# The last adds and their output transfers moved into the LSTM's pass loop

## The reference

```python
lstm_out = _lstm(layernorm(x))                 # 8192 steps, hidden 128
g = argmax(lstm_out @ W_lin.T + b_lin)         # 0 or 1 per step
w = g * lstm_out
inc = cumsum(w)
prefix, suffix = inc - w, inc[-1] - inc
x + 2.0 * lstm_out + prefix * fw_att + suffix * bw_att
```

## Time and profile before

| | us |
|---|---|
| median of 3 runs (lowest, highest) | 1605.08 (1603.58, 1605.31) |
| profiled execution | 1600.95 |
| its span | 1598.9 |
| PE busy | 1511.9 |
| DVE busy | 1369.9 |
| POOL busy | 1123.2 |
| ACT busy | 1040.0 |
| repeated steps of the pass loop | about 1462 to 1574 |
| behind them, to the span's end | 1574 to 1598.9 |

### The profile page before, as it was taken

One profiled execution on the slowest core, in us unless ns is written; L12 is line 12 of the kernel. 1 busy time (PEld: TensorE's weight loads), 2 busy tenths in 40 slices (PEclk: granted clock), 3 DMA queues, 4 the chain that ended last, 5 costly groups with the idle time before them and its releaser, 6 DMA issues. The chain is left out here.

```text
span 1598.9 us, 17964 instructions
## 1 busy us (share of the span) xinstructions
PE 1511.9 (95%) x5006; PEld 772.3 (48%) x5006; DVE 1369.9 (86%) x1623; ACT 1040.0 (65%) x2210; POOL 1123.2 (70%) x536
## 2 busy tenths in 40 slices
PE   8999999999999999999999999999987688999994
PEld 3444444444444444444444444444432235998993
DVE  7406999999999999999999999999988695667998
ACT  3254766667676767675767666676768666777772
POOL 0325989898989898898989898989898761001221
PEclk9999999999999999999999999999989899999997
DMA  9877767677776776777777777776720203000002
GB/s 368 332 251 260 263 225 250 241 254 248 248 262 232 254 246 239 236 253 262 244 254 246 252 249 248 258 243 239 254 97 9 99 1 119 0 0 1 0 0 105
DMA packets 60491, 313.51 MB, mean 196 GB/s; under 512 B 6492, under 2 KB 6544, under 8 KB 27525
## 3 DMA queue, kind: packets, MB, share of 16 engines
q1 hardware_dynamic: 49537, 293.30, 52.8%
q10 hardware_dynamic: 10884, 19.41, 3.8%
HBM read 300.36 MB, written 12.32 MB: 196 GB/s over the span
## 5 line engine op out<-in xcount | busy, mean ns | idle before, releaser
L586 PE MATMUL bank<-ring,xh 128*128 128x512 f32 x2048 | 956.3, 594 | 13.2 <-DVE xh L1179 7.9
L1295 DVE TENSOR_TENSOR_SCAN work<-bank,hstate,work 128x512 f32<-128x512 f32 x512 | 628.1, 1268 | 29.9 <-ACT bank L881 24.4
L586 PEld LDWEIGHTS bank<-ring,xh 128*128 128x128 f32 x2048 | 387.9, 190 | 464.6 <-issue 422.6
L1065 POOL TENSOR_TENSOR work<-work 128x1024 f32<-128x1024 f32 x210 | 495.5, 2359 | 85.6 <-DVE work L1244 77.2
L881 ACT ACTIVATE bank<-work,a_neg 128x512 f32<-128x512 f32 x512 | 344.3, 686 | 226.1 <-DVE work L1295 225.4
L1236 DVE TENSOR_TENSOR work<-work,bank 128x1024 f32<-128x1024 f32 x256 | 310.1, 1217 | 62.0 <-POOL work L1041 50.8
L1244 DVE TENSOR_TENSOR work<-work,bank 128x1024 f32<-128x1024 f32 x168 | 201.2, 1198 | 20.8 <-POOL work L1065 20.8
L480 PE MATMUL bank<-bc_parts,sel 96*128 96x512 bf16 x456 | 172.0, 386 | 28.1 <-DVE work L1236 12.8
L475 PE MATMUL bank<-work,w_sb 128*128 128x512 f32 (+2 forms) x352 | 178.1, 602 | 5.9 <-ACT work L795 2.7
L1140 POOL TENSOR_TENSOR work<-work 128x256 f32 x32 | 28.6, 894 | 215.5 <-ACT work L944 215.5
L1010 POOL TENSOR_TENSOR work<-work 128x1024 f32<-128x1024 f32 x48 | 113.5, 2365 | 18.9 <-ACT work L755 18.7
(11 more groups left out here) (153 smaller groups left out, 1595.4 us busy)
## 6 DMA issues: line engine op xcount, KB each, us to landing
ring<-adj_t SPq DMA_DIRECT2D x256, 1024.0 KB, 5.6
work<-c_scratch ACTq DMA_DIRECT2D x28, 256.0 KB, 5.5
c_two<-c_scratch ACTq DMA_DIRECT2D x28, 256.0 KB, 5.1
xh<-x_rows SPq DMA_DIRECT2D x16, 256.0 KB, 7.0
work<-x_t SPq DMA_DIRECT2D x16, 256.0 KB, 5.4
x_scratch<-work ACTq DMA_DIRECT2D x16, 256.0 KB, 3.8
work<-x_scratch SPq DMA_DIRECT2D x1, 4096.0 KB, 14.1
out_t<-work SPq DMA_DIRECT2D x16, 256.0 KB, 2.4
```

The costliest lines, as they stand in the source:

```text
L586: last = nc.tensor.matmul(mixed[:, :], xn[:, j, :], a, start=(j == 0), stop=(j == BLK - 1))
L1065: nc.gpsimd.tensor_tensor(out=acc, in0=hc[0] if n == 1 else acc, in1=hc[n % 2], op=ALU.add).then_inc(y_added, 1)
L1295: nc.vector.tensor_tensor_scan(hb[s % 2][:, h, :], da[h], dbu[s % 2][:, h, :], hstate[:, HV * s + h:HV * s + h + 1], ALU.mult, ALU.add).th ...
```

## The change

The sixteen last adds move into the While loop: DVE makes eleven of them (chunks 0 to 10), GpSimd five (chunks 11 to 15). For DVE the values are also written to PSUM (`k_bank`), and its adds read them there; GpSimd reads `k_seg` in SBUF. SP gets a While loop of its own, in which it sends the 16 chunks in the order `OUT_ORDER` as they are ready, loads the flag ahead of the last one, and waits for all transfers at the loop's end. In every step GpSimd now also waits that the chunks of the pass before are out (`out_done`, met at once in the first pass). The copies of the states and the count of passes move from the end of the pass to its head, which takes the place of L1337 to L1339; PE's wait for `guess_ready` moves into its loop. The tail's side operations are ordered anew: both selects stand among the comparisons, the rest behind them, `flag` comes later and `k_seg` right behind it.

```diff
@@ -72,6 +72,9 @@
           ("out", 11.5, "post"), ("pcen", 12.5, "post"), ("pvar", 13.5, "post")]
 O_SHARED = 9
 POOL_HC = (1, 3, 8, 10)
+POOL_OUT = (11, 12, 13, 14, 15)
+DVE_OUT = tuple(i for i in range(NC) if i not in POOL_OUT)
+OUT_ORDER = (0, 1, 11, 2, 3, 12, 4, 5, 13, 6, 7, 14, 8, 9, 15, 10)
 C_LOAD = {0: 1, 2: 3, 6: 8, 8: 10}
 PRE_STEPS = sum(s[2] == "pre" for s in SHARED)
 POST_STEPS = sum(s[2] == "post" for s in SHARED)
@@ -252,6 +255,11 @@
         at[0] = pre_only
         o_in = [carve(N // BG).rearrange("p (c t) -> p c t", c=NC // BG) for _ in range(BG)]
+        def last_sum(i, k):
+
+            return (final[:, i, :].rearrange("p (t s) -> p t s", s=SPC),
+                    k[:, i * SPC:(i + 1) * SPC].unsqueeze(1).broadcast_to([P, SEG, SPC]))
+
         def by_chunk_seg(ap):
             return ap.rearrange("p (c s) -> p c s", s=SPC)
@@ -277,6 +285,7 @@
         out_gate = [bank[4], bank[5]]
         l_bank = [bank[6], bank[7]]
         count_ps = bank[6][:, NSEG:NSEG + 1]
+        k_bank = bank[7][:, NSEG:2 * NSEG]
         o_bank = [bank[2]] * O_SHARED + [bank[i] for i in (7, 1, 3, 7, 6, 7, 6)]
...
@@ -410,10 +419,26 @@
             sp.wait_ge(x1_stored, 16 * NC)
             sp.wait_ge(xl_ready, NC)
             sp.dma_start(x1_all, x1_dram.rearrange("c p t -> p c t")).then_inc(x1_in, 16)
-            for i in range(NC):
-                sp.wait_ge(out_ready, i + 1)
-                sp.dma_start(out_t[i], final[:, i, :]).then_inc(out_done, 16)
-            sp.wait_ge(out_done, 16 * NC)
+            sp.sem_inc(out_done, 16)
+            pass_no = sp.alloc_register("sp_pass")
+            go_on = sp.alloc_register("sp_go")
+            sp.reg_mov(pass_no, 0)
+            sp.reg_mov(go_on, 1)
+            with sp.While(lambda: sp.snap(go_on)):
+                pn = sp.snap(pass_no)
+                for i in OUT_ORDER:
+                    if i == OUT_ORDER[-1]:
+                        sp.wait_ge(flag_ready, pn + 1)
+                        sp.sem_inc(flag_seen, 1)
+                        sp.reg_load(go_on, flag[0:1, 0:1])
+                    if i in POOL_OUT:
+                        sp.wait_ge(out_pool, len(POOL_OUT) * pn + (POOL_OUT.index(i) + 1))
+                    else:
+                        sp.wait_ge(out_ready, len(DVE_OUT) * pn + (DVE_OUT.index(i) + 1))
+                    sp.dma_start(out_t[i], final[:, i, :]).then_inc(out_done, 16)
+                sp.wait_ge(out_done, 16 * NC * pn + (16 * NC + 16))
+                sp.sem_inc(flag_seen, 1)
+                sp.reg_add(pass_no, pass_no, 1)
         @block.tensor
@@ -683,9 +708,9 @@
             run_steps(SEG - WARM, -2 * (SEG - WARM), from_zero=True)
             for b in range(2):
                 input_part(0, 0, b)
-            pe.wait_ge(guess_ready, 1)
             with pe.While(lambda: pe.snap(go_on)):
                 pn = pe.snap(pass_no)
+                pe.wait_ge(guess_ready, pn + 1)
                 run_steps(0, 2 * SEG * pn + 2 * WARM, earlier=SEG * pn)
                 pe.wait_ge(hid_ready, 2 * SEG * pn + 2 * (WARM + SEG))
                 logits(SEG - 1, 1, SEG * pn)
@@ -1137,8 +1162,14 @@
                     for e in range(2):
                         cols = bass.ds((t + e) * SPC, SPC)
                         pool.wait_ge(h2_ready, SEG * pn + (t + e + 1))
+                        pool.wait_ge(out_done, 16 * NC * pn + 16)
                         nc.gpsimd.tensor_tensor(out=final[:, :, cols], in0=by_chunk_seg(h2[e]), in1=x1_all[:, :, cols],
                                                 op=ALU.add).then_inc(a_ready, 1)
+                pool.wait_ge(k_ready, pn + 1)
+                pool.wait_ge(fin_ready, SEG * pn + SEG)
+                for i in POOL_OUT:
+                    o, add = last_sum(i, k_seg)
+                    nc.gpsimd.tensor_tensor(out=o, in0=o, in1=add, op=ALU.add).then_inc(out_pool, 1)
                 pool.wait_ge(flag_ready, pn + 1)
                 pool.sem_inc(flag_seen, 1)
                 pool.reg_load(go_on, flag[0:1, 0:1])
@@ -1333,13 +1364,8 @@
                 for e in range(2):
                     cell_step(t + e, e, 2 * (t + e) - 2 * (SEG - WARM))
-            dve.wait_ge(hid_ready, 2 * WARM)
-            nc.vector.tensor_copy(hs[:, 0, 1:NSEG], hs[:, SEG, 0:NSEG - 1])
-            link(nc.vector.tensor_copy(c_in[:, 1:NSEG], c_st[:, 0:NSEG - 1]))
-            nc.vector.tensor_copy(c_st, c_in).then_inc(guess_ready, 1)
             dve.sem_inc(wsel_ready, 2)
             dve.wait_ge(x1_stored, 16 * NC)
-            dve.wait_ge(guess_ready, 1)
             links_before = n[0]
             with dve.While(lambda: dve.snap(go_on)):
                 pn = dve.snap(pass_no)
@@ -1379,6 +1405,14 @@
                     ins.then_inc(check_step, 1)
                     dve.wait_ge(check_step, base + k[0])
+                E = NSEG - 1
+                dve.wait_ge(hid_ready, hid_base)
+                nc.vector.tensor_copy(hs[:, 0, 1:NSEG], hs[:, SEG, 0:E])
+                then(nc.vector.tensor_copy(c_in[:, 1:NSEG], c_st[:, 0:E]))
+                nc.vector.tensor_copy(c_st, c_in).then_inc(guess_ready, 1)
+                dve.wait_ge(guess_ready, pn + 1)
+                then(nc.vector.tensor_scalar(passes, passes, 1.0, None, ALU.add))
+                nc.vector.tensor_scalar(alive, passes, float(NSEG), None, ALU.is_lt)
                 nc.vector.memset(cum[1], 0.0).then_inc(cum_ready, 1)
                 cell_step(0, 0, hid_base)
                 cell_step(1, 1, hid_base + 2)
@@ -1389,43 +1423,42 @@
                         cell_step(t + e, e, hid_base + 2 * (t + e), side(t + (e - 2), e))
                 dve.wait_ge(hid_ready, hid_base + 2 * SEG)
-                E = NSEG - 1
+                select(SEG - 2, 0)
                 nc.vector.tensor_tensor(out=diff[:, E:2 * E], in0=c_st[:, 0:E], in1=c_in[:, 1:NSEG], op=ALU.subtract)
                 then(nc.vector.tensor_tensor(out=diff[:, 0:E], in0=hs[:, SEG, 0:E], in1=hs[:, 0, 1:NSEG], op=ALU.subtract))
+                select(SEG - 1, 1)
                 then(nc.vector.tensor_tensor(out=diff, in0=diff, in1=diff, op=ALU.mult))
                 nc.vector.tensor_tensor(out=diff[:, E:2 * E], in0=diff[:, E:2 * E], in1=c_tol, op=ALU.is_le)
                 then(nc.vector.tensor_scalar(diff[:, 0:E], diff[:, 0:E], TOL * TOL, None, ALU.is_le))
                 nc.vector.reduce_sum(agree, diff, axis=AX.X).then_inc(agree_ready, 1)
-                nc.vector.tensor_copy(hs[:, 0, 1:NSEG], hs[:, SEG, 0:E])
-                then(nc.vector.tensor_scalar(passes, passes, 1.0, None, ALU.add))
-                nc.vector.tensor_scalar(alive, passes, float(NSEG), None, ALU.is_lt)
-                then(nc.vector.tensor_copy(c_in[:, 1:NSEG], c_st[:, 0:E]))
-                nc.vector.tensor_copy(c_st, c_in)
+                for last in (SEG - 2, SEG - 1):
+                    accumulate(last, last % 2)
+                    dve.wait_ge(cum_ready, SEG * pn + pn + (last + 2))
+                nc.vector.tensor_tensor_scan(inc[:, 1:1 + NSEG], cum[1], cum[1], inc[:, 0:1], ALU.add,
+                                             ALU.bypass).then_inc(inc_ready, 1)
+                own_term(SEG - 2, 0)
+                own_term(SEG - 1, 1)
+                dve.wait_ge(inc_ready, pn + 1)
+                nc.vector.tensor_tensor(out=bw_total, in0=inc[:, NSEG:1 + NSEG], in1=V("bw"), op=ALU.mult).then_inc(total_ready, 1)
+                sum_term(SEG - 2, 0)
+                sum_term(SEG - 1, 1)
                 dve.wait_ge(agree_sum, pn + 1)
                 nc.vector.scalar_tensor_tensor(out=flag[:, :], in0=count_ps[0:1, :], scalar=float(2 * E * P),
                                                in1=alive[0:1, :], op0=ALU.is_lt, op1=ALU.mult).then_inc(flag_ready, 1)
-                for last in (SEG - 2, SEG - 1):
-                    for part in side(last, last % 2):
-                        part()
-                nc.vector.tensor_tensor_scan(inc[:, 1:1 + NSEG], cum[1], cum[1], inc[:, 0:1], ALU.add,
-                                             ALU.bypass).then_inc(inc_ready, 1)
-                dve.wait_ge(inc_ready, pn + 1)
-                nc.vector.tensor_tensor(out=bw_total, in0=inc[:, NSEG:1 + NSEG], in1=V("bw"), op=ALU.mult).then_inc(total_ready, 1)
                 dve.wait_ge(total_ready, pn + 1)
                 nc.vector.tensor_scalar(k_seg, inc[:, 0:NSEG], fwbw, bw_total, ALU.mult, ALU.add).then_inc(k_ready, 1)
-                dve.wait_ge(k_ready, pn + 1)
+                nc.vector.tensor_scalar(k_bank, inc[:, 0:NSEG], fwbw, bw_total, ALU.mult, ALU.add).then_inc(k_placed, 1)
+                dve.wait_ge(k_placed, pn + 1)
                 dve.wait_ge(fin_ready, SEG * pn + SEG)
+                for i in DVE_OUT:
+                    o, add = last_sum(i, k_bank)
+                    nc.vector.tensor_tensor(out=o, in0=o, in1=add, op=ALU.add).then_inc(out_ready, 1)
                 dve.wait_ge(flag_ready, pn + 1)
                 dve.sem_inc(flag_seen, 1)
```

(5 more changed lines are left out.)

4 lines of the change are left out of this document (2 added, 2 removed).

## The result

| us | before | after |
|---|---|---|
| median (lowest, highest), 20 runs each | 1603.43 (1600.44, 1605.65) | 1601.61 (1598.49, 1602.84) |
| ratio of the two, 95% interval | | 0.9985 (0.9979 to 0.9992) |
| profiled execution, its span | 1600.95, 1598.9 | 1600.21, 1598.4 |

By the ratio the change saves 2.4 us, between 1.3 and 3.4; the two medians differ by 1.8. The forecast was 2.0 less, and 1603.1 on a base of 1605.08. The base itself measured 1.65 lower this time, and that alone is more than the 1.5 between 1603.1 and 1601.61.

The account below looks back on a forecast made before the run. The tail from the first issue was taken as a full-rate DMA transfer, so the first add's start decides the end. Terms -2.74 - 0.25 + 0.7 + 0.3 = -2.0 took 1605.08 to 1603.1 us, range 1600.6 to 1605.8.

Parts of the forecast that it names:

- tail up to the first add (H to F): From the pass's last hidden state (H) to DVE's first last add (F): 2.74 us less.
- head (W to P): From the warm-up's last hidden state (W) to PE's first loop matmul (P): 0.25 us less, bounds 0.05 to 0.5.
- loop's steps, GpSimd's wait (P to H): First loop matmul to last hidden state: GpSimd's extra wait holds DVE, 0.3 us more, bounds 0 and 3.1.
- SP's loop exit: At the very end, SP adds, branches back, compares and leaves: 0.7 us more, bounds 0.3 and 2.7.
- five adds by GpSimd: Last adds: chunks ready in 7.1 us instead of 9.7, but the DMA engines want 10.4; counted as nothing.
- the last landing behind F (the flag's load, code fetches): After the first last add: flag load ahead of the sixteenth chunk hidden by chunks in flight; no cost counted.
- the first rival: Last adds: the adds, not the DMA, end the tail, -5.8 us there, 1600.0 in all; chance 7%.
- the 0.98 for the copies: Tail: L1399 to L1403 leave it, 0.98 us less, part of the 2.74.
- the third rival: SP's back branch: a code fetch costs 2.0 us more than taken, 1605.1 in all; chance 8%.
- The second: Last adds: DVE and GpSimd hold each other, DMA engines end 2.0 us later, 1605.1; chance 6%.
- the case within 0.2%: Whole kernel: the measurement can't tell the time from no change, within 0.2% or 3.2 us; chance 67%.

Follow-up runs that it names:

- e11: Kernel before with only the change's head part (copies and counts at the loop's head, PE's wait in its loop): ratio 1.0000.
- e7: Changed kernel with three more, already met, semaphore waits for GpSimd in each step: first loop matmul to last hidden state 122.14 us instead of 120.07.
- e6: e4 with SP's wait for all transfers moved behind its loop: ratio 0.9981 to the kernel before, first last add to span's end 13.38 us.
- e4: Changed kernel with SP loading the flag ahead of its first chunk instead of its last: ratio 0.9989 to the kernel before.
- e1: Changed kernel with all sixteen last adds by DVE, chunks sent in order 0 to 15: ratio 0.9986 to the kernel before.
- e5: Changed kernel with SP's loop and flag load replaced by straight code, valid for one pass: first last add to span's end 13.03 us, against 14.02.
- e3: Changed kernel sending only half of each chunk: first last add to span's end 12.19 us, 1.8 less.
- e8: Changed kernel with the comparison behind DVE's last adds and SP's flag load behind its last issue: ratio 0.9964 to the kernel before.
- e9: e8 with SP's wait for all transfers moved behind its loop: ratio 0.9967 to the kernel before.
- e10: e9 with all sixteen last adds by DVE: ratio 0.9985 to the kernel before.
- e12: e9 with PE making the first step's twelve input products twice to fill its idle time: ratio 0.9958 to the kernel before, median 1596.63 us.
- e2: Changed kernel with DVE's adds reading k in SBUF instead of PSUM: ratio 1.0007 to the kernel before.

## Why the prediction was right, point by point

| term | predicted | measured | by |
|---|---|---|---|
| tail up to the first add (H to F) | -2.74 | -2.89 | after |
| head (W to P) | -0.25 | -0.23 | after, e11 -0.22 |
| loop's steps, GpSimd's wait (P to H) | +0.3 | -0.19 | after, e7 |
| SP's loop exit | +0.7 | +0.6 | after, e6 against e4 |
| five adds by GpSimd | 0 | 0 | e1 |
| the last landing behind F (the flag's load, code fetches) | 0 | +0.6 | after (12.99, before 12.42), e5 |
| sum | -2.0 | -2.1 | |

*The bound.* "From the first issue to the end the tail is a DMA transfer at full rate" held: the rate is unchanged, GpSimd's share is worth nothing (e1), and half the bytes end 1.8 earlier (e3). What the reading missed is that the next bound is not 5 us away, as the first rival had it by the adds' time, but under 2, at SP's issues.

*The tail.* The count of operations was right to 0.15. One of its pieces rests on more than the count: the 0.98 for the copies is real only because other work stands in their place while PE sums the verdict (e11: 0.12 without it). The prediction didn't say so.

*The loop's steps.* Wrong in sign, by 0.5. (That DVE is the bound there doesn't follow from its 105.21 busy us in the earlier trace rows: PE has 109.65 in the same row. The chain of waits of the kernel before shows it: from 1480 to 1540 DVE's lines are two thirds of it, and none of its twelve largest lines is PE's.) The step read GpSimd's end from its start plus a fixed duration. The duration isn't fixed: the add starts under DVE's sum term and ends 0.58 to 0.60 behind it in both kernels. Alone it has 0.73, so it could start up to 0.13 ahead of the sum term's end, some 0.2 later than it did before, and end no later. e7 uses that up. Why P to H came out 0.19 shorter was not tested; 0.14 of it lies in the last 28 steps (104.67 before, 104.53 after), and the interval of the runs is far too wide for it.

*SP.* The exit was right. Put at nothing was all else behind F, and it cost 0.6: the last landing comes 12.99 behind F instead of 12.42. Hidden was to be the flag's load ahead of the sixteenth chunk; it took 1.08 us with the queues full, more than the few chunks in flight cover, and left a hole at 1595.38. Moving it (e4) closed the hole but gave only 0.1, since behind it stood a cost that the prediction had nowhere: each fetch of code beside the transfers holds, as the counts have it, one DMA engine and with it the last landing. Two fetches cost 0.5 (e4, e6), the single one 0.25 in e5 and 0.5 to 0.7 in e8, e9, e10 and e12. These rest on one profile each, but the counts agree in all nine of the table.

*The rivals.* None came. No fetch stands at SP's back branch: from the branch that closes the loop to SP's next instruction are 0.3 us in every kernel with that loop, so the third rival's 2.0 isn't there. Fetches did matter, but on the DMA engines, beside the transfers. The second, the hold between DVE and GpSimd, was priced at 2.0 behind the first add; with k in SBUF it costs 3.6 (e2), since GpSimd's adds lose time too. The Trainium skill's rule (SBUF — State Buffer, "Who interferes with whom") is borne out by the pair: eleven adds take 11.78 us with two SBUF inputs beside GpSimd and 6.67 with one of them in PSUM. In the pass loop a held add has some 0.13 us done by the end of the operation that holds it (0.73 less 0.60).

*The range.* The median after, 1601.61, lies in it, 1.5 below the forecast, and the ratio, 0.15% less, is the case within 0.2% that had the most weight. The base moved by 1.65. The terms are off by 0.1 together, but that is luck: the loop came out 0.5 lower and the last landing 0.6 higher than forecast, and the two cancel.

The transfers' bound points to the better version: what must not stand ahead of the first issue is the comparison, and what must not stand behind the last landing is a loop's exit. e9 does both and ends 19.44 us behind the last hidden state, the kernel before 24.87; e12 adds PE's filling and has the best median and interval, -6.7 us (-8.8 to -4.5).

## What to carry to other kernels

When a tail is bound by its transfers, count only what stands ahead of the first issue and behind the last landing; how fast the chunks are made matters when something else queues behind their making, as the comparison did in e10. What runs beside a full queue isn't free either: there a load of one word took 1.1 us, and fetches of code held the last landing back. An operation removed from ahead of a wait is worth its time only if something else covers the wait. And cut two profiles at common events before comparing them: here one stretch, the same code in all, has two lengths 1.7 apart, by TensorE's granted clock.
